# Two scan products behind each other in every second step, in an attention-like layer on one core

## The reference, cut to what matters

```python
proj = hidden_states @ in_proj_w.T
gate, xBC, dt = jnp.split(proj, [INTER, INTER + CONV_DIM], axis=-1)
...
xBC = jax.nn.silu(jnp.swapaxes(conv, 1, 2))         # after a causal convolution of 4 taps
x, Bm, Cm = jnp.split(xBC, [INTER, INTER + NG * SS], axis=-1)
...
scores = jnp.einsum('bclhn,bcshn->bchls', Cc, Bc) * Lmat
Ydiag = jnp.einsum('bchls,bcshp->bclhp', scores, xdt)
...
Y = (Ydiag + Yoff).reshape(Bsz, S, H, P) + x * D[None, None, :, None]
...
yg = y * jax.nn.silu(gate)
rstd = jax.lax.rsqrt(jnp.mean(jnp.square(yg_g), axis=-1, keepdims=True) + EPS)
out = (yg_g * rstd).reshape(Bsz, S, INTER) * norm_w
return out @ out_proj_w.T
```

## Time and profile before

| | us |
|---|---|
| median of 3 runs | 1622.42 (1621.36 to 1623.8) |
| profiled execution | 1622.23 |
| its span | 1619.7 |
| PE busy | 1599.7 (99%) |
| DVE busy | 1410.6 (87%) |
| ACT busy | 1197.0 (74%) |
| POOL busy | 959.1 (59%) |

### The profile page before, as it was taken

One profiled execution on the slowest core, in us unless ns is written; L12 is line 12 of the kernel. 1 busy time (PEld: TensorE's weight loads), 2 busy tenths in 40 slices (PEclk: granted clock), 3 DMA queues, 4 the chain that ended last, 5 costly groups with the idle time before them and its releaser, 6 DMA issues.

```text
span 1619.7 us, 28500 instructions
## 1 busy us (share of the span) xinstructions
PE 1599.7 (99%) x8500; PEld 1268.2 (78%) x8500; DVE 1410.6 (87%) x1652; ACT 1197.0 (74%) x2305; POOL 959.1 (59%) x594
## 2 busy tenths in 40 slices
PE   9999989999999999999999999999999999999998
PEld 6777767877778777887778878787788777877776
DVE  7735799889898899889898899889898899889987
ACT  4523888778787877878787877877887878778772
POOL 6422355666566655765575655666666656656563
PEclk9999999999999999999999999999999999999999
DMA  5233344433443335334443435333443444434432
GB/s 169 79 117 134 108 140 152 138 128 129 138 154 128 126 119 177 118 132 131 150 147 112 138 125 166 129 121 131 145 152 109 148 132 146 137 114 154 157 133 83
DMA packets 83719, 216.48 MB, mean 134 GB/s; under 512 B 10576, under 2 KB 12880, under 8 KB 83424
## 3 DMA queue, kind: packets, MB, share of 16 engines
q1 hardware_dynamic: 83264, 214.15, 40.0%
q10 hardware_dynamic: 288, 0.30, 0.1%
HBM read 209.43 MB, written 4.98 MB: 132 GB/s over the span
## 4 chain that ended last, share of the span: by engine, by line
PE 88%; DVE 6%; issue 2%; ACT 2%; POOL 1%; DMA 0%; ACTq 0%; DVEq 0%; SPq 0%; POOLq 0%
PE pj L450 16%; PE pj L452 15%; PE pj L451 15%; PE pr L450 9%; PE pr L451 8%; PE pr L452 8%; PE sc L670 7%; PE sc L674 3%; PE tb L659 3%; DVE conv L1321 2%; DVE wo_lo L1385 1%; PE pr L648 1%; PE tb L683 1%; ACT decay L928 1%; DVE xc L1335 1%
## 5 line engine op out<-in xcount | busy, mean ns | idle before, releaser
L1028 POOL TENSOR_TENSOR w_lo<-stg,w_hi 128x512 fp32r<-128x512 f32 x316 | 494.9, 1567 | 335.3 <-ACT w_hi L902 262.7
L450 PE MATMUL pj<-xT_hi,w_hi 128*128 128x512 f32 x1208 | 477.4, 395 | 9.8 <-DVE conv L1321 5.3
L452 PE MATMUL pj<-xT_hi,w_lo 128*128 128x512 f32 x1208 | 470.9, 390 | 0.0
L451 PE MATMUL pj<-xT_lo,w_hi 128*128 128x512 f32 x1208 | 470.4, 389 | 0.0
L1321 DVE SCALAR_TENSOR_TENSOR conv<-pj,par,conv 128x510 f32<-128x510 f32 (+2 forms) x480 | 357.9, 746 | 77.7 <-ACT conv L910 64.4
L928 ACT ACTIVATE decay<-decay,dtg 128x256 f32<-128x256 f32 (+1 forms) x1024 | 379.0, 442 | 0.0
L1063 POOL TENSOR_TENSOR xc<-xc,thg 128x512 f32<-128x512 f32 x128 | 203.1, 1587 | 188.1 <-DVE xc L1372 187.8
L1069 POOL TENSOR_TENSOR sqsum<-sqsum,sq 128x512 f32<-128x512 f32 x112 | 218.1, 1948 | 113.7 <-ACT sq L954 110.3
L450 PEld LDWEIGHTS pj<-xT_hi,w_hi 128*128 128x128 f32 x1208 | 226.7, 188 | 68.0 <-issue 15.7
L452 PEld LDWEIGHTS pj<-xT_hi,w_lo 128*128 128x128 f32 x1208 | 226.8, 188 | 48.1
L451 PEld LDWEIGHTS pj<-xT_lo,w_hi 128*128 128x128 f32 x1208 | 226.9, 188 | 45.1
(11 more groups left out here) (182 smaller groups left out, 2005.9 us busy)
## 6 DMA issues: line engine op xcount, KB each, us to landing
stg<-wstream SPq DMA_DIRECT2D x387, 256.0 KB, 2.7
decay<-cs_scr SPq DMA_DIRECT2D x128, 768.0 KB, 4.3
acc<-hid SPq DMA_DIRECT2D x8, 256.0 KB, 5.0
out<-acc SPq DMA_DIRECT2D x8, 256.0 KB, 2.0
dt_scr<-decay SPq DMA_DIRECT2D x1, 1024.0 KB, 6.3
gate_scr<-part SPq DMA_DIRECT2D x4, 256.0 KB, 2.0
dtg<-dt_scr SPq DMA_DIRECT2D x16, 64.0 KB, 4.0
stg<-hid SPq DMA_DIRECT2D x4, 256.0 KB, 4.0
```

Source lines behind the costliest of these rows:

```text
L450: nc.tensor.matmul(dst, hi_w, hi_x, start=first, stop=False)
L451: nc.tensor.matmul(dst, hi_w, lo_x, start=False, stop=False)
L452: return nc.tensor.matmul(dst, lo_w, hi_x, start=False, stop=last)
L1028: nc.gpsimd.tensor_tensor(w_dest(n, 1), stg[:, s % RING, :], f32(w_dest(n, 0)), ALU.subtract).then_inc(S["wl"], 1)
```

## The change

Scans are issued only in steps with an odd number, two behind each other: pairs `s - 1` and `s`. The sum of an even pair goes to `sc` as before, that of an odd pair to another bank: `tb` in pair 1, `pr[0]` in pair 3, and `pr[3]` in pairs 5 and 7. As pair 1's sum lies in the bank in which x is turned, pair 2 is turned at the end of step 1, after the output product. PE has new waits: the scan of pair 1 for `mean_square`, those of pairs 3, 5 and 7 for `add_output` of their `pr` bank, output products 0 and 3 for the `add_scan` that frees their bank, and the turn of pair 2 for the `add_scan` of pair 1. The four other programs get a new order to go with it: on DVE both `add_scan` come in odd steps, both `y_lo` in even ones, and `add_output` of bank 3 at the head of step 5; on ACT both `y_hi` and both `square` come in even steps, the second square behind `decays`; on POOL both `gated` come in odd steps, both `add_square` in even ones, the second behind the low parts of the weights. Arithmetic and amounts are the same.

```diff
+        yb = [sc, tb, sc, pr[0], sc, pr[3], sc, pr[3]]
...
             def x_turn(g, half, j):
...
+                if j == 2:
+                    pe.wait_ge(S["u"], at(g, half, NJ, 2))
...
             def scan(g, half, j):
...
-                pe.wait_ge(S["u"], at(g, half, NJ, j))
+                pe.wait_ge(S["u"], at(g, half, NJ, j - 1))
+                if j == 1:
+                    pe.wait_ge(S["ms"], at(g, half, 1, 0))
+                elif j % 2 == 1:
+                    pe.wait_ge(S["acc"], at(g, half, 4, 1 if j == 3 else 4))
...
+                if t in (0, 3):
+                    pe.wait_ge(S["u"], at(g, half, NJ, 4 if t == 0 else NJ))
...
-                if has_pair(g, half, s + 1):
+                if s != 1 and has_pair(g, half, s + 1):
                     x_turn(*pair(g, half, s + 1))
-                if has_pair(g, half, s):
+                if s % 2 == 1 and has_pair(g, half, s):
+                    scan(g, half, s - 1)
                     scan(g, half, s)
...
                 if with_out:
                     out_of_step(g, half, s)
+                if s == 1:
+                    x_turn(*pair(g, half, s + 1))
```

ACT, in `step` (`done` is the list of the two pairs whose scans came in the step before, in even steps):

```diff
-                if s >= 1 and has_pair(g, half, s - 1):
-                    y_hi(g, half, s - 1)
-                    square(g, half, s - 1)
+                if done:
+                    y_hi(*done[0])
+                    square(*done[0])
+                    y_hi(*done[1])
                 if has_pair(g, half, s + 2):
                     drops(*pair(g, half, s + 2), 1)
...
                 if has_pair(g, half, s + 2):
                     decays(*pair(g, half, s + 2))
+                if done:
+                    square(*done[1])
```

POOL and DVE, in `step`:

```diff
                 if with_out and s == 0:
-                    add_square(*before, NJ - 1)
+                    add_square(*before, NJ - 2)
...
                 for i in range(1, n):
                     split_low(g, half, s, i)
-                if has_pair(g, half, s):
+                if with_out and s == 0:
+                    add_square(*before, NJ - 1)
+                if s >= 2 and s % 2 == 0 and has_pair(g, half, s):
+                    add_square(g, half, s - 1)
+                if s % 2 == 1 and has_pair(g, half, s):
+                    gated(g, half, s - 1)
                     gated(g, half, s)
...
+                if with_out and s == 5:
+                    add_output(*before, 3)
...
-                if has_pair(g, half, s):
+                if s % 2 == 1 and has_pair(g, half, s):
+                    add_scan(g, half, s - 1)
                     add_scan(g, half, s)
...
-                if s >= 1 and has_pair(g, half, s - 1):
-                    y_lo(g, half, s - 1)
+                if s >= 2 and s % 2 == 0 and has_pair(g, half, s - 1):
+                    y_lo(g, half, s - 2)
...
+                if s >= 2 and s % 2 == 0 and has_pair(g, half, s - 1):
+                    y_lo(g, half, s - 1)
+                if s == 0 and with_out:
+                    y_lo(*before, NJ - 1)
...
             finish(2)
             finish(3)
+            y_lo(G - 1, 1, NJ - 2)
+            finish(4)
             y_lo(G - 1, 1, NJ - 1)
-            finish(4)
```

More of the change, by code:

```diff
@@ L669, in scan @@
                         hd = slice(h * HD, (h + 1) * HD)
-                        nc.tensor.matmul(sc[hd, c0:c0 + 2 * P], xdt[:, j % 2, 2 * b, hd],
+                        nc.tensor.matmul(yb[j][hd, c0:c0 + 2 * P], xdt[:, j % 2, 2 * b, hd],
                                          decay[:, j % NDEC, 2 * h + b, 0:2 * P], start=True, stop=False)
@@ L673, in scan @@
                         hd = slice(h * HD, (h + 1) * HD)
-                        mm = nc.tensor.matmul(sc[hd, c0 + P:c0 + 2 * P], xdt[:, j % 2, 2 * b + 1, hd],
+                        mm = nc.tensor.matmul(yb[j][hd, c0 + P:c0 + 2 * P], xdt[:, j % 2, 2 * b + 1, hd],
                                               decay[:, j % NDEC, 2 * h + b, 2 * P:3 * P], start=False, stop=True)
@@ L968, in step @@
                     drops(*pair(g, half, s + 2), 0)
-                if s >= 1 and has_pair(g, half, s - 1):
-                    y_hi(g, half, s - 1)
-                    square(g, half, s - 1)
+                before = (g, 0) if half == 1 else (g - 1, 1)
                 if s == 0 and with_out:
-                    before = (g, 0) if half == 1 else (g - 1, 1)
-                    y_hi(*before, NJ - 1)
-                    square(*before, NJ - 1)
+                    done = [(*before, NJ - 2), (*before, NJ - 1)]
+                elif s >= 2 and s % 2 == 0 and has_pair(g, half, s - 1):
+                    done = [(g, half, s - 2), (g, half, s - 1)]
+                else:
+                    done = []
+                if done:
+                    y_hi(*done[0])
+                    square(*done[0])
+                    y_hi(*done[1])
                 if has_pair(g, half, s + 2):
@@ L1010, in _ @@
                 step(G - 1, 1, s)
-            y_hi(G - 1, 1, NJ - 1)
-            square(G - 1, 1, NJ - 1)
+            for j in (NJ - 2, NJ - 1):
+                y_hi(G - 1, 1, j)
+                square(G - 1, 1, j)
         @block.gpsimd
@@ L1076, in step @@
                 if with_out and s == 0:
-                    add_square(*before, NJ - 1)
+                    add_square(*before, NJ - 2)
                 if with_out and s == 2:
                     inverse_rms(*before)
-                if s >= 2 and has_pair(g, half, s):
-                    add_square(g, half, s - 1)
+                if s >= 4 and s % 2 == 0 and has_pair(g, half, s):
+                    add_square(g, half, s - 2)
                 for i in range(1, n):
                     split_low(g, half, s, i)
-                if has_pair(g, half, s):
+                if with_out and s == 0:
[4 more added lines that the diff above has]
+                    gated(g, half, s - 1)
                     gated(g, half, s)
@@ L1101, in _ @@
                 step(G - 1, 1, s)
+            add_square(G - 1, 1, NJ - 2)
             add_square(G - 1, 1, NJ - 1)
@@ L1372, in add_scan @@
                 nc.vector.scalar_tensor_tensor(out=xc[:, j, :], in0=xc[:, j, :], scalar=par[:, C_DV + j:C_DV + j + 1],
-                                               in1=sc[:, :], op0=ALU.mult, op1=ALU.add).then_inc(S["u"], 1)
+                                               in1=yb[j][:, :], op0=ALU.mult, op1=ALU.add).then_inc(S["u"], 1)
             def y_lo(g, half, j):
@@ L1418, in step @@
                     mask_products(*following(g, half))
-                if has_pair(g, half, s + 1):
+                if s % 2 == 0 and has_pair(g, half, s + 1):
                     x_times_dt(*pair(g, half, s + 1))
-                if has_pair(g, half, s):
+                if s % 2 == 1 and has_pair(g, half, s):
+                    add_scan(g, half, s - 1)
                     add_scan(g, half, s)
+                if s % 2 == 1 and s != 1 and has_pair(g, half, s + 1):
+                    x_times_dt(*pair(g, half, s + 1))
                 for m in mine[1:]:
                     taps(g, half, m)
-                if s >= 1 and has_pair(g, half, s - 1):
-                    y_lo(g, half, s - 1)
+                if s >= 2 and s % 2 == 0 and has_pair(g, half, s - 1):
+                    y_lo(g, half, s - 2)
                 if s == 0 and with_out:
-                    y_lo(*before, NJ - 1)
+                    y_lo(*before, NJ - 2)
                 if mine:
@@ L1434, in step @@
                     split_out_lo(g, half, s)
-                if with_out and 2 <= s <= 5:
+                if with_out and 2 <= s <= 4:
                     add_output(*before, s - 2)
```

## The result

| | before | changed |
|---|---|---|
| median | 1622.08 us (1621.36 to 1623.8, 4 runs) | 1642.7 us (1639.54 to 1645.33, 4 runs) |
| ratio | | 1.0121, 95% interval 1.0109 to 1.0133 |
| profiled execution, span | 1622.23, 1619.7 | 1643.84, 1642.0 |

What follows compares the result with a forecast made beforehand. PE, busy 99% of the span, sets the pace, with DVE close behind. Against 1622.23 us: -13.8 (PE's gain) + 17.2 + 2.1 (square sums) + 1.3 (tail) = +6.8, so 1629.0 us; range 1610 to 1641.

Steps and rivals of the forecast that it cites:

- PE's gain: Pairing scans on PE saves array tiling changes: net 13.8 us (11 to 20), 0.87 for each half.
- Entry and exit of the scans: Changing PE to 64 columns and back costs 0.09 + 0.05 + 0.10 = 0.24 us; 64 scans save it, 15.6 us.
- The turn alone: A turn without a scan behind it, step 1: pays 0.11 us on PE's first matmul, 1.8 us over 16 halves.
- The square sums: PE waits for the later last square and POOL's addition: 17.2 us at half 0 to 1, 2.1 at half 1 to 0.
- the step I lean on most: PE's square-sum line waits for POOL's sqsum, 2 us at most half-0-to-1 passages.
- The loads: Even pairs' exponents, with weight pieces queued behind on SP, land up to 1 us late for ACT; PE's work covers that.
- What costs nothing: New waits for u and acc, gate_tanh's later gated, and later exponents and weight pieces were all taken as covered.
- rival 3: Late loads delay ACT's gates; PE stops 1 us more in two three-block steps of half 0: 1645 us, chance 0.05.
- PE's work of three blocks covers that: In even steps, loads landing up to 1 us after ACT would like them were to cost PE nothing.
- Step 4 of half 0: PE stops 0.1 to 1 us at the second x block for the gate block's bank; not added again to square sums.
- The tail: After the last scan, products needing y_lo of pair 6 wait behind two finish pairs: 1.3 us lost (0 to 2).
- Size: Loss of 1.35 + 0.8 = 2.15 us in each of eight passages from half 0 to half 1.

Runs made afterwards that it cites:

- experiment 7: Changed kernel with two weight pieces ahead of the exponents, B and C products behind the scans, y_lo of pair 6 early: 1604.81 us, 0.9892 of the kernel before.
- experiment 1: Changed kernel with an even pair's exponents issued one step later on SP, behind the first two weight pieces: 1613.23 us, 0.994 of the kernel before.
- 3: Changed kernel loading only the first head's exponents of each pair (384 KB instead of 768): 1625.25 us, ratio 1.0013 to the kernel before.
- 4: Control: the kernel before, loading only the first head's exponents of each pair: 1622.59 us, ratio 0.9995.
- 2: The kernel before with only the exponents of even pairs issued as late as in the changed kernel: 1625.23 us, ratio 1.0009.
- 5: Changed kernel, loads still late, with step 5's B and C products behind turn and scans, their masking behind x_times_dt: 1626.68 us, ratio 1.0022.
- experiment 6: Changed kernel with y_lo of pair 6 ahead of the two finish pairs at the end: 1639.62 us, ratio 1.0105 to the kernel before.

## Why the prediction was wrong, point by point

- **PE's gain**, forecast 13.8 us (0.87 a half): measured 1.1 to 1.2 a half with next to no stall in it, 18 to 19 us. Entry and exit of the scans were right. The turn alone was priced too high: 0.35 us and a next block of 2.85 against 2.72, 0.48 in all, where I had 0.55. Five such turns stand in each half.
- **The square sums**, 17.2 and 2.1 us, "the step I lean on most": this step failed. They do wait, in 14 of 15 passages of the changed kernel, but for 0.17 us in the mean and 2.4 us in all, which the list of waits doesn't show. The passage at 1009, ACT, POOL and then PE, where the two starts lie 0.40 apart instead of 0.23:

```profile
1006.81 0.61 ACT L970 ACTIVATE sq<-xc 128x512 f32<-128x512 f32 x1
1007.58 1.29 POOL L1092 TENSOR_TENSOR sqsum<-sqsum,sq 128x512 f32<-128x512 f32 x1 [0.36 <-ACT sq L970]
1008.61 0.39 PE L455 MATMUL pj<-xT_hi,w_lo 128*128 128x512 f32 x1
1009.01 0.38 PE L693 MATMUL tb<-cst,sqsum 128*128 128x1 f32 x2
```

  The new place of the square is as I had it (it starts 1.38 us after the exponentials do). That PE comes late from its stalls isn't what spares it. In experiment 7 the pieces are in time and PE has its whole gain, and the sums wait only 0.2 us in all 15 passages together. One of them, with the sums at 986.85:

```profile
984.57 0.62 ACT L975 ACTIVATE sq<-xc 128x512 f32<-128x512 f32 x1
985.35 1.29 POOL L1097 TENSOR_TENSOR sqsum<-sqsum,sq 128x512 f32<-128x512 f32 x1 [0.35 <-ACT sq L975]
986.62 0.39 PE L460 MATMUL pj<-xT_hi,w_lo 128*128 128x512 f32 x1
```

  Two terms were wrong. From the end of the exponentials to the sums I had 2.55 us, and took off 0.87 for PE's gain, 0.52 for the second y_hi and 0.8 for lateness, which leaves 0.36; in experiment 7 it is 2.1 to 2.3 in this kind of passage. So ACT kept up with PE; why, the runs don't separate. And the addition, for which I took 1.27 to 2.61, took 1.29 or 1.30 in every passage (in this kind of passage 1.30 to 1.40 before as well, which I could have read): from the end of the exponentials the sums need 2.1 us.
- **The loads**, under "What costs nothing" and as rival 3 at 0.05: "PE's work of three blocks covers that" was the wrong sentence. I had the mechanism and an estimate of up to 1 us; ACT waited 2.3 us in the mean of 52 times. My estimate let exponents and pieces land one behind the other, but not that three pieces and the next exponents are issued within 2.4 us, where they had been spread over a step. And I followed the lateness only to the gate blocks (5.2 us in the trace, as rival 3 has it in small), not through the tap of the second x block and two x_silu to the B and C products. There one wait sat in 13 of 14 steady halves: 9.6 us of the 10.9 listed (the other 1.3 is in the first half, and in the kernel before too), 16 us when it is removed. Rival 3 gave 1645 us, near the 1642.7, for 1 us in each of two gate waits of half 0, which is not where the time went; its size is luck.
- **Step 4 of half 0**, a stall of 0.1 to 1 us at the second x block: it is there once in seven halves (0.68 us). Waits of this kind stand in steps 4 and 6 of both halves, seven in the steady part, 3.3 of the 5.2 us listed. I counted it as a part of the square sums' loss; with the pieces in time (experiment 1) none is left there.
- **The tail**, 1.3 us: 3.7 us listed. The instructions of the finish pairs and y_lo itself took up to 1.75 us instead of 0.7 while POOL worked, and I had taken only y_lo's place in line. What I had not thought of came after it: 1.7 us more, by a lower clock (below).
- **The start**: the new wait of turn 2, 3.4 us once, was in the diff, and I priced it for the steady state, with an output product in front of it. The first half has none. Behind it another 1.4 us went at the lower clock (below).
- **Size.** The lost time comes to 2.1 us a half in the 14 intervals (1.0 of net loss, in which the one fall of the clock has 0.1, and 1.1 of eaten gain), in both halves. I had 2.15 in every second one. The sum was close to right per passage by chance, for another place and half as often.

Shown by runs: that the late pieces are the cause (1, 3, 4), that late loads alone, in the old order, cost next to nothing (2), and that the B and C products are the main place where they reach PE (5). Not separated: what in the new order takes the cover away, the missing scan or the longer lists; what part of the 29 us in experiment 1 is the pieces, and what the exponents' own lateness.

## What to carry to other kernels

When two pieces of work on the bounding engine are put together, the steps between them get shorter, and buffers come free later and in pairs: look first at what the load queue does with that, and put the small loads that the next step begins with ahead of the large one that has to wait. Follow a lateness through every engine to its last consumer, not just to the next wait of the bounding engine; a product whose inputs come last can often move behind work that is ready. And price each new wait at the first and the last step, where the cover of the steady state is missing. A wait of 0.2 us can be missing in a list of waits; the distance between two starts shows it.

## What the runs showed of the hardware that was not expected

After the wait of 3.7 us at the tail, PE's matmuls came every 0.43 us instead of 0.23 for about three us. Windows of the changed kernel (the granted clock is the number behind POOL's):

```profile
1600.00:1622.00 22.00, 18.46 (x103) 14.40 (x101) 19.00 (x21) 6.12 (x11) 12.83 (x8) 1.00 0.14 50
1622.00:1623.50 1.50, 1.30 (x5) 1.06 (x6) 1.47 (x4) 0.00 (x0) 0.00 (x0) 0.82 0.00 0
1623.50:1626.50 3.00, 3.00 (x9) 2.37 (x8) 1.87 (x3) 0.00 (x0) 0.00 (x0) 0.52 0.23 87
```

The granted clock is at its lower level, 1.2 GHz, and at 2.4 GHz again by 1626.6. The 18 matmuls before the last square sums took 5.8 us from 1622.2, where they took 4.08 before: 1.7 us, nearly half of the wait on top of it. In experiment 6, with the wait gone, the stretch is 6.2 us shorter.

The same fall comes twice more in this execution: at 196.5, in the wait of 3.4 us for turn 2, and in the steady part, behind the longest wait for the B and C products. PE at that wait, and the windows of both falls:

```profile
1512.34 0.70 PE L651 MATMUL pr<-bc 128*128 128x256 f32 x2 [1.84 <-DVE bc L1364]
196.50:199.50 3.00, 2.76 (x9) 2.40 (x10) 3.00 (x4) 2.18 (x6) 3.00 (x3) 0.50 1.02 412
1514.00:1517.00 3.00, 3.00 (x18) 1.91 (x18) 2.96 (x4) 0.39 (x1) 0.38 (x1) 0.50 0.02 5
```

Each lasted about 3.4 us. At half the pace that is 1.4 us lost behind the first, which began in the wait itself, and 1.7 behind each of the others: some 5 of the 22.3 us of span. The kernel before had none while PE worked. The length of the wait alone does not tell which: the changed kernel's waits of 1.42 and 1.66 us at 222 and 227 brought no fall, nor did the wait of 3.46 us for turn 2 in experiment 6 (its granted clock from 197 to 200 is 1.00). The four runs of the changed kernel differ in the same sense: 1639.54 us at a mean clock of 0.998, 1643.84 and 1641.56 at 0.996, 1645.33 at 0.995. The stalls of under 1 us in the steady state brought no fall: the clock was 1.00 in the interval from 1009.01 to 1099.97.

Four transposes with an ordinary matmul behind them cost nothing beside their own work: 0.35 us to its start and 0.32 to the next one are 0.67, and four times 0.11 and once 0.23 are 0.67. After a scan or the square sums the same first matmul costs 0.11 more.
